# x sums of two row tiles ahead of the query product, five warm-up products, and projection weights stored as rows of 512

## What is computed

```python
# conditioned layer: v is x, W3 is 256 x 512, W2 is 512 x 512
q_emb = jax.nn.relu(q @ W3 + b3)
v_sum = jnp.sum(v, axis=1, keepdims=True)
h0 = jax.nn.relu(((n * v + v_sum) * q_emb[:, None, :]) @ W2 + b2)
# feed-forward layer: W_fc is 2048 x 512, W_proj is 512 x 2048
w1 = _ternary_weight(W_fc, GROUP)      # per 64 numbers of a row: scale * (-1, 0 or 1)
h = jnp.square(jax.nn.relu(jnp.einsum('bsd,hd->bsh', h0, w1)))
w2 = _ternary_weight(W_proj, GROUP)
out = x + jnp.einsum('bsh,dh->bsd', _rms_norm(h), w2)
```

## Time and profile before

| what | us |
|---|---|
| median of three runs | 323.41 |
| lowest and highest of them | 322.25, 323.43 |
| profiled execution | 322.98 |
| its span, first to last instruction | 321.0 |
| PE busy | 315.2 |
| DVE busy | 210.6 |
| ACT busy | 192.3 |
| POOL busy | 112.9 |

### The profile page before, as it was taken

The page is one execution under the profiler, slowest core; times in us unless marked ns, Lnnn a source line. Parts: engine busy times, 40 slices in busy tenths (PEclk is TensorE's granted clock), DMA queues, the critical chain, the costliest instruction groups (busy, mean ns, idle before and its releaser), DMA issues.

```text
span 321.0 us, 3855 instructions
## 1 busy us (share of the span) xinstructions
PE 315.2 (98%) x1336; PEld 239.8 (75%) x1336; DVE 210.6 (66%) x290; ACT 192.3 (60%) x282; POOL 112.9 (35%) x94
## 2 busy tenths in 40 slices
PE   8999999999999999999999999999999999999995
PEld 7764554644888788888888888888888888888884
DVE  0447989798998856577555565855565575665545
ACT  1639898799996876444555444554445554445550
POOL 1003333334553435414334441334443314443330
PEclk9999999999999999999999999999999999999999
DMA  6993959678731110007000000510000015000003
GB/s 190 300 315 84 267 157 255 172 146 263 130 52 34 33 36 1 0 0 263 0 0 2 0 0 0 198 68 0 2 0 0 0 64 199 0 0 2 0 1 132
DMA packets 31331, 27.02 MB, mean 84 GB/s; under 512 B 18736, under 2 KB 20816, under 8 KB 31312
## 3 DMA queue, kind: packets, MB, share of 16 engines
q1 hardware_dynamic: 29984, 26.25, 29.8%
q10 hardware_dynamic: 1328, 0.53, 0.6%
HBM read 18.39 MB, written 4.19 MB: 70 GB/s over the span
## 4 chain that ended last, share of the span: by engine, by line
PE 69%; ACT 10%; DVE 7%; issue 7%; DMA 5%; SPq 0%; POOL 0%; DVEq 0%; ACTq 0%; POOLq 0%
PE ps_out L321 34%; PE ps_acc L308 31%; DMA w_turned<-w_tern 3%; DVE abs_sum L412 3%; DMA raw<-in_L_ffn_W_proj_dram 3%; DVE x_t L439 2%; ACT w_scale L532 2%; ACT h_f L554 2%; PE ps_acc L363 1%; ACT x_t L562 1%; ACT w_abs L526 1%; ACT x_t L559 1%; PE ps_out L273 1%; ACT w_t L539 1%; ACT w_sign L527 1%
## 5 line engine op out<-in xcount | busy, mean ns | idle before, releaser
L210 POOL TENSOR_TENSOR wv_sb<-wv_sb 128x512 f32<-128x512 f32 x55 | 82.2, 1494 | 113.9 <-ACT wv_sb L565 113.9
L321 PE MATMUL ps_out<-w_t,y_hi 128*128 128x512 f32 x256 | 101.7, 397 | 0.2 <-DVE y_lo L454 0.2
L321 PE MATMUL ps_out<-w_t,y_lo 128*128 128x512 f32 x256 | 100.9, 394 | 0.0
L308 PE MATMUL ps_acc<-h_hi,w_t 128*128 128x512 f32 x256 | 100.1, 391 | 0.0
L308 PE MATMUL ps_acc<-h_lo,w_t 128*128 128x512 f32 x256 | 100.0, 391 | 0.0
L454 DVE TENSOR_TENSOR y_lo<-x_t,y_hi 128x512 fp32r<-128x512 f32 x64 | 91.3, 1427 | 2.2
L559 ACT ACTIVATE x_t<-ps_acc 128x512 f32<-128x512 f32 x64 | 38.1, 595 | 81.0 <-PE ps_acc L308 81.0
L452 DVE CAST y_hi<-x_t 128x512 fp32r<-128x512 f32 x64 | 29.5, 461 | 73.2 <-PE ps_out L321 65.7
L321 PEld LDWEIGHTS ps_out<-w_t,y_hi 128*128 128x128 f32 x256 | 48.1, 188 | 11.7 <-DVE y_lo L454 0.6
L321 PEld LDWEIGHTS ps_out<-w_t,y_lo 128*128 128x128 f32 x256 | 48.3, 189 | 10.9
L308 PEld LDWEIGHTS ps_acc<-h_hi,w_t 128*128 128x128 f32 x256 | 48.3, 189 | 10.6 <-issue 0.2
(11 more groups left out here) (48 smaller groups left out, 148.7 us busy)
## 6 DMA issues: line engine op xcount, KB each, us to landing
x_sb<-in_x_dram SPq DMA_DIRECT2D x7, 1024.0 KB, 6.3
raw<-in_L_ffn_W_fc_dram SPq DMA_DIRECT2D x8, 512.0 KB, 5.7
raw<-in_L_ffn_W_proj_dram SPq DMA_DIRECT2D x8, 512.0 KB, 6.1
out_dram<-x_t SPq DMA_DIRECT2D x16, 256.0 KB, 2.5
x_sb<-in_x_dram SPq DMA_DIRECT2D x4, 256.0 KB, 5.6
wv_sb<-in_L_cond_W_dram SPq DMA_DIRECT2D x4, 256.0 KB, 7.2
x_t<-in_L_cond_W_dram ACTq DMA_DIRECT2D x1, 512.0 KB, 4.9
w_turned<-w_tern SPq DMA_TRANSPOSE x16, 3.1
```

The source lines that it names most:

```text
L210: engine.tensor_tensor(sq_acc[:], sq_acc[:], y_sq[:, v % SQ_RING, :], ALU.add).then_inc(sq_added, 1)
L308: last = pe.matmul(ps_acc[:, (UNITS + v) % ACC_RING, :], w_t[:, j, k * P:(k + 1) * P], part[:, k, g * BANK:(g + 1) * BANK], start=(k == 0 ...
L321: last = pe.matmul(ps_out[:, t, :], part[:, v % RING, t * P:(t + 1) * P], w, start=(j == 0 and part is y_hi), stop=(j == HJ - 1 and part i ...
```

## The change

Three things. WARM_UP goes from 10 to 5. The query product moves from ahead of the x sums of group 0 to between those of tile 1 and those of tile 2. And the projection weights lie otherwise in w_t: row 16 + j holds all 512 outputs of hidden block j, so project reads one run of 512 numbers; keep_pair, which fills these rows, writes eight runs of 128 numbers where it wrote 1024 numbers in a row. The hidden weights are kept as before.

```diff
-WARM_UP = 10
+WARM_UP = 5
...
-                c, i = j // TT, j % TT
-                w = w_t[:, HJ + KD * c:HJ + KD * (c + 1), i * P:(i + 1) * P]
+                w = w_t[:, HJ + j, :]
...
-            pe.wait_ge(condt_ready, 1)
-            pe.wait_ge(wq_loaded, 16)
-            for m in range(KD):
-                for k in range(KQ):
-                    last = pe.matmul(ps_x[:, m * BATCHES:(m + 1) * BATCHES], wq_sb[:, k, m * P:(m + 1) * P],
-                                     cond_t[:, k, :], start=(k == 0), stop=(k == KQ - 1))
-            last.then_inc(q_done, 1)
             pe.wait_ge(consts_ready, 1)
             for t in range(TT):
+                if t == TT // 2:
+                    pe.wait_ge(condt_ready, 1)
+                    pe.wait_ge(wq_loaded, 16)
+                    for m in range(KD):
+                        for k in range(KQ):
+                            last = pe.matmul(ps_x[:, m * BATCHES:(m + 1) * BATCHES], wq_sb[:, k, m * P:(m + 1) * P],
+                                             cond_t[:, k, :], start=(k == 0), stop=(k == KQ - 1))
+                    last.then_inc(q_done, 1)
                 pe.wait_ge(x0_loaded[t], 16)
...
-                act.activation(w_t[:, at:at + 2, :].rearrange("p i w -> p (i w)"),
-                               w_turned[:].rearrange("p b w -> p (b w)"), ACT.Copy).then_inc(wt_ready, 1)
+                if at < HJ:
+                    act.activation(w_t[:, at:at + 2, :].rearrange("p i w -> p (i w)"),
+                                   w_turned[:].rearrange("p b w -> p (b w)"), ACT.Copy).then_inc(wt_ready, 1)
+                else:
+
+                    c, first = (at - HJ) // KD, (at - HJ) % KD * P
+                    act.activation(w_t[:, HJ + TT * c:HJ + TT * (c + 1), first:first + 2 * P].rearrange("p j (i w) -> p i j w", i=2),
+                                   w_turned[:].rearrange("p (i j) w -> p i j w", i=2), ACT.Copy).then_inc(wt_ready, 1)
```

## The result

The changed kernel takes 321.12 us, the median of seven runs (320.74 to 321.67), the kernel before 323.28 us in its seven (322.25 to 323.61). The ratio is 0.9942 with a 95% interval of 0.9926 to 0.9959: faster, by 0.58% or 1.9 to 2.2 us. Forecast were 319.5 us. The time lies in the stated range, but 1.6 us of the promised gain are missing.

What follows compares the result with a forecast made beforehand. PE, busy 315.2 of 321.0 us, and the weight preparation were taken to bind. From 322.98 us, 1.2 for the start and 2.3 for the layout gave 319.5 us; the range was 318.3 to 322.6 us.

Steps and rivals of the forecast that it cites:

- What bounds the kernel: PE and the weight preparation both bind; both start from the end of the x sums of group 0.
- Contiguous projection weights: Project line: one run of 512 instead of four saves 0.04 us in each of 58 groups, 2.3 us.
- The copies: ACT's eight copies of projection pairs, now writing runs of 128, stay at 1050 ns: no gain or cost taken.
- Five warm-up products fewer: PE's start: 2.17 us of weight loads go, 0.8 and 0.15 us given back at the lower clock level.
- The moved query product: Behind tile 1's x sums it avoids a 0.8 us wait for w_q, counted within the sum for PE's start.
- The third rival: PE pauses at tile 1, the clock rises only behind the x sums: slower, 326.8 us with eight slow h0 records; chance 0.07.
- Does the shift arrive at the weights?: DMA loads: the 1.2 us shift fits a 1.3 us traffic hole; raw weights land at 20.9 instead of 22.15 us.
- the head: PE's start up to h0, with shorter warm-up and moved query product: gain 1.2 us, bounds 0.4 to 1.6.
- The first rival: Project line: runs are free, 0.04 us comes from y as stationary operand; only the start counts, 321.8 us; chance 0.22.

Runs made afterwards that it cites:

- e13_y_phase: The changed kernel with y_hi and y_lo allocated ahead of abs_sum and scale, so 128 bytes lower: 318.38 us, ratio 0.9876 to the kernel before.
- e10_y_still: The changed kernel, but from tile 16 on DVE writes its split of y to the idle tile raw; project-line groups still 1.86 us.
- e18_phase_runs: The kernel before, old layout, with y_hi and y_lo placed like w_t within 256 bytes, moved query product, three warm-up products: 318.17 us, ratio 0.9868.

## Why the prediction was wrong, point by point

**What bounds the kernel** held: both PE and the weight preparation start with the x sums of group 0, and a shift of that start reached the end.

**Contiguous projection weights** failed, and this is the step that was wrong: "So I put the 0.04 us on the four runs". The cost per group was real, the 58 groups and their place on the path too. But of three differences between the lines one was excluded by rows, and of the other two the changed one was taken, though nothing spoke against the stationary operand but the form of its load. Its term of 2.3 us measured 0 (the layout alone: ratio 1.0005). The rule of the Trainium skill that was set beside it (SBUF — State Buffer, section Specifications (TRN2): lines of 16 bytes, each cross to a new one costs) allowed for runs of 128 numbers to be free, and they are. The 0.04 us came from y's place in SBUF, 128 bytes off that of the moving w_t. Put right, it gives about the forecast gain. A pair of groups goes from 3.68 to 3.62 us, since the step from the hidden line to the project line gets shorter too. From the first project group behind y_lo to PE's end the chains of the changed kernel and of the one with y moved take 209.9 and 207.0 us, 2.9 us less:

```profile
311.62 3.84 PE ps_out L320 x16
```

```profile
105.44 2.12 PE ps_out L320 x8
...
308.63 3.81 PE ps_out L320 x16
```

The first row ends the changed kernel, the other two are those of e13_y_phase. Between runs the gain is 2.1 us by the two ratios to the kernel before (0.9942 and 0.9876), and 2.7 us between the medians (321.12 and 318.38), which were not taken side by side.

**The copies** held: 1048 ns in the median in the new form, against 1050.

```profile
L545 ACT ACTIVATE w_t<-w_turned x8: 1042/1048/1065, 38.2 to 115.2; 128x1024 fp32r<-128x1024 bf16 x8
```

**Five warm-up products fewer**: the mechanism held, with h0 at 11.88 us instead of the forecast 12.0. The x sums of tile 0 went at the lower level, 0.8 us given back as reckoned. That it came so near is luck in part. "If the level rises at the same moment" was taken from one execution; in the profiled executions without a late rise, the first weight load of 192 ns comes anywhere from 5.1 to 8.3 us. In e10_y_still, with the same start as the changed kernel, the sums of tiles 0 and 1 took 3.36 us instead of 2.70, and h0 began at 12.54 us:

```profile
5.32 3.36 PE L273 MATMUL ps_out<-sum_mat,x_sb 128*128 128x128 f32 x16
```

**The moved query product** was right in its times (7.86 us, 1.87 us long) and wrong in its worth. The prediction has "the move saves that wait", 0.8 us for w_q. Without the move the wait was 0.40 us, and the query product started before the level rose; h0 then came at 15.47 us and not at 11.88, 3.6 us later. The two edits are worth something only together. The third rival had this mechanism, a late rise, at another place: it asked for a pause at tile 1, and the pause of 0.32 us there in e18_phase_runs did no harm.

**Does the shift arrive at the weights?** Yes, and with more than forecast: this term was too small. 1.2 us were forecast for the head; the start of h0 gave 1.36 us, and 0.6 us came on the way to 107.52 us, where PE is 1.98 us ahead. Of these, 0.48 us arise up to x of group 2: the raw weights landed 2.3 and not 1.2 us earlier, issued 1.36 us earlier and landed after 7.2 instead of 8.2 us, so PE's wait there went. The prediction had left the length of this transfer as it was. An earlier start alone did not bring it: in the profiled execution of the layout alone the level rose early and h0 began at 12.19 us, yet the raw weights took 8.1 us and PE waited 0.51 us for x of group 2. The three kernels with ten warm-up products show 8.1 to 8.3 us, all with fewer 6.9 to 7.5 us, the one with the warm-up shortened and nothing else among them (7.2). Why is open.

The first rival, the runs free and the 0.04 us from y as stationary operand, is what happened. It gave 321.8 us; the rest to 321.12 is the head's larger term.

## What to carry to other kernels

A difference in pace between two lines of code names no cause: list all in which they differ, and before costing the one that is to be changed, exclude the others by an experiment that changes each alone. Where stationary and moving operands of a matmul come from tiles of different size, put the small tiles behind the large ones, so that all operands of TensorE lie at the same place within 512 bytes; here moving two lines of allocations gave as much as the whole change beside it, 2.1 to 2.9 us. And shorten a warm-up only together with the order of what follows it.

## What the runs showed of the hardware

A matmul of 512 columns in float32r (fp32r in the rows) goes every 227 ns when the stationary and the moving tile lie at the same place within 512 bytes, and about every 233 when they lie 128 bytes apart: groups of 8 of the project line at 1.81 us in all six kernels of the first kind (two of them with w_t or h0 as stationary operand, which lie right), at 1.86 in every one of the second. Other distances, and whether 256 or 512 bytes is the period, were not tried. The step from the last hidden product to the first project product went with it: the hidden line, whose operands lay right all along, is at 1.82 us beside a wrong neighbour and 1.81 beside a right one.

The clock rose to the 2.4 GHz level at different times with the same work ahead of it. With ten warm-up products the first load of 192 ns came at about 7.4 us in the kernel before and at 5.1 us in the run with the layout alone, whose 20 warm-up records took 4.14 and not 4.64 us. With the start of the changed kernel it came from 5.3 us (e13_y_phase) to 8.3 us (e10_y_still). It rose at 13.5 us or later in the three profiled executions in which the query product began at the lower level. The granted clock read 1.00 in these windows; only the length of the weight loads and the distance of the records showed it.
